# A gated MLP with adapters: gate and up by seven block products for two token tiles, samples in four quarters

## The reference

```
x = x + L0(x, itok_B_1_198)          # einsum('bct,bcd->bdt', x, weights[conditions])
x = x + L1(x, itok_B_0_7)
x = x + L2(x, itok_B_0_7) + bias
def _lora_linear(x, W, A, B, adapter_indices):
    base = jnp.einsum('bsd,df->bsf', x, W)
    lora = jnp.einsum('bsr,brf->bsf', jnp.einsum('bsd,bdr->bsr', x, Ai), Bi)
    return base + lora
h = jax.nn.silu(gate) * up           # 512 -> 2048
x = x + _lora_linear(h, Wd, Ad, Bd, adapter_indices)   # 2048 -> 512
```

## Time and profile before

| | us |
|---|---|
| median of 3 runs | 1435.89 (1435.2 to 1436.04) |
| span of the profiled execution | 1433.6 |
| TensorE busy | 1398.0 |
| DVE busy | 737.1 |
| ACT busy | 289.9 |
| POOL busy | 823.5 |

### The profile page before, as it was taken

How to read it: one execution, slowest core, us unless ns; L and a number is a source line. 1 busy time by engine, 2 the same in 40 slices (tenths; PEclk the granted TensorE clock), 3 DMA queues, 4 the chain that set the end, 5 groups by cost and what they waited for, 6 DMA issues and landing times.

```text
span 1433.6 us, 19764 instructions
## 1 busy us (share of the span) xinstructions
PE 1398.0 (98%) x6822; PEld 1177.2 (82%) x6822; DVE 737.1 (51%) x1212; ACT 289.9 (20%) x545; POOL 823.5 (57%) x854
## 2 busy tenths in 40 slices
PE   4999999999999999999989999999999999999997
PEld 4788888888888888888878888888888888888886
DVE  6885444454544545454574545445445445445456
ACT  3422211111222212122222211111111111111111
POOL 5764666666667666666642265555555555555550
PEclk7999999999999999999999999999999999999999
DMA  6522332323232232223245122222222222222213
GB/s 208 201 84 62 107 94 86 93 84 97 82 95 87 82 100 81 91 87 95 86 152 173 45 79 65 83 81 66 78 82 72 76 82 66 77 79 67 73 59 118
DMA packets 62968, 131.72 MB, mean 92 GB/s; under 512 B 13904, under 2 KB 18768, under 8 KB 62928
## 3 DMA queue, kind: packets, MB, share of 16 engines
q0 software_dynamic: 26624, 70.29, 15.5%
q1 hardware_dynamic: 36304, 60.90, 13.4%
HBM read 113.97 MB, written 17.17 MB: 91 GB/s over the span
## 4 chain that ended last, share of the span: by engine, by line
PE 94%; DVE 5%; issue 1%; DMA 0%; ACT 0%; SPq 0%; DVEq 0%; ACTq 0%
PE pd L1170 25%; PE pu L1170 25%; PE pg L1170 25%; PE pv L1170 7%; PE pu L1257 4%; PE pg L1257 3%; PE px L1170 2%; DVE acc L1058 1%; PE pu L1232 1%; DVE w_lo L884 1%; DMA bias_src<-bias_t 0%; DVE acc L1048 0%; PE px L1232 0%; DVE xt_lo L898 0%; PE pg L1311 0%
## 5 line engine op out<-in xcount | busy, mean ns | idle before, releaser
L485 POOL DMA_INDIRECT b_got<-b_table,idx_b x480 | 486.8, 1014 | 152.0 <-issue 115.7
L1027 DVE TENSOR_TENSOR h<-silu,pu 128x512 f32<-128x512 f32 x128 | 87.9, 687 | 620.3 <-PE pu L1257 620.3
L542 POOL TENSOR_TENSOR h_lo<-h,h_hi 128x512 fp32r<-128x512 f32 x128 | 166.5, 1301 | 373.6 <-ACT h_hi L648 372.4
L1058 DVE TENSOR_TENSOR acc<-pd,acc 128x512 f32<-128x512 f32 x512 | 348.4, 689 | 2.9 <-PE pd L1170 1.5
L1170 PE MATMUL pd<-w_hi,h_hi 128*128 128x512 f32 x512 | 207.2, 405 | 2.5 <-DVE acc L1058 2.5
L1170 PE MATMUL pg<-xt_hi,w_hi 128*128 128x512 f32 x528 | 208.4, 395 | 0.2 <-DVE xt_lo L898 0.2
L1170 PE MATMUL pg<-xt_hi,w_lo 128*128 128x512 f32 x528 | 206.1, 390 | 0.0
L1170 PE MATMUL pu<-xt_hi,w_hi 128*128 128x512 f32 x512 | 205.9, 402 | 0.0
L1170 PE MATMUL pg<-xt_lo,w_hi 128*128 128x512 f32 x528 | 205.9, 390 | 0.0
L1170 PE MATMUL pd<-w_lo,h_hi 128*128 128x512 f32 x512 | 200.0, 391 | 0.0
L1170 PE MATMUL pu<-xt_lo,w_hi 128*128 128x512 f32 x512 | 199.9, 390 | 0.0
(11 more groups left out here) (216 smaller groups left out, 1735.0 us busy)
## 6 DMA issues: line engine op xcount, KB each, us to landing
w_raw<-w_all SPq DMA_DIRECT2D x96, 256.0 KB, 2.7
b_got<-b_table,idx_b POOLq DMA_INDIRECT x480, 2.8
out<-acc SPq DMA_DIRECT2D x7, 1024.0 KB, 5.0
acc<-x SPq DMA_DIRECT2D x4, 1024.0 KB, 8.4
xn<-x SPq DMA_DIRECT2D x16, 256.0 KB, 2.7
x_next<-xn SPq DMA_DIRECT2D x16, 256.0 KB, 2.8
acc<-x_next SPq DMA_DIRECT2D x4, 1024.0 KB, 5.9
w_raw<-w_all SPq DMA_DIRECT2D x32, 64.0 KB, 1.9
```

What stands on the lines that cost most here:

```text
L485: gp.indirect_dma_start(out=dst, out_offset=None, in_=table, in_offset=bass.IndirectOffsetOnAxis(ap=rows.bitcast(U32), axis=0)).then_inc(s ...
L542: gp.tensor_tensor(h_lo[:, slot, :], h[:, :], h_hi[:, slot, :], ALU.subtract).then_inc(h_lo_done, 1)
L1027: dve.tensor_tensor(h[:, :], silu[:, :], pu[slot][:, :], ALU.mult).then_inc(h_done, 1)
L1058: dve.tensor_tensor(dst, psum[:, :], dst, ALU.add).then_inc(down_add, 1)
```

## The change

Samples are worked in four quarters of 8 pairs, two tiles each. A unit is one hidden block for both tiles of a quarter; the adapter products are a unit of their own (block -1), so a quarter has 17 units. Seen as 2 x 2 blocks (two tiles by two halves of the 512 inputs, times two halves by gate and up), gate and up of both tiles are eight block products. Now there are seven, made from sums and differences of token blocks (`xo_hi`, `xo_lo`: A11, S1, A12, S2, A22_T3, S3, A22) and of weight blocks (`sums` on DVE, for each unit). Some are added in PSUM (`px` takes four of them in turn), and ACT copies and DVE additions in between (`s1_kept`, `s5_kept`, `s2_kept`, `c11_done`, `u3_done`, `c12_done`, `c22_done`, `c21_kept`) form gate and up of tile 0 in `g0`, `up0` and of tile 1 in `g1`, `up1`. The products' marks p1, p5, p6, p2, p7, p3, p4 follow in this order on TensorE. Down products wait for two blocks and are added in PSUM over both: after an odd block tile 0, after the next even one tile 1, so a unit still has 30 of them and 5 additions. Weights are read and split four times instead of twice. The pairs of the next quarter are prepared in units 2 to 9 (`gather_pair`, L424 for all gathers), four turns (transposes and token sums) in units 5, 7, 9 and 11; the sums go to `xops` in DRAM and come back in unit 15. ACT waits for `b_out` (the stores of `b_table`) before the first turn of the opening. The loops are written out in full.

```diff
+QP = PAIRS // QUARTERS
+TP = QP // 2
 TOK = TP * P
...
+SUPER = BLOCKS // 2
...
+UNITS = BLOCKS + 1
...
+A11, S1, A12, S2, A22_T3, S3, A22 = range(7)
+S4 = A22_T3
...
+                if b == BLOCKS - 1 and q + 1 < QUARTERS:
+                    sp.wait_ge(xops_out, TP * (q + 1) * 16)
+                    for done, k in ((p1_mm, A11), (p5_mm, S1), (p6_mm, S2), (p2_mm, A12), (p7_mm, S3), (p3_mm, S4),
+                                    (p4_mm, A22)):
+                        sp.wait_ge(done, n + 1)
+                        for c in range(2):
+                            src = xops[:, :, k * WH + c * P:k * WH + (c + 1) * P].rearrange("j p n -> p j n")
+                            sp.dma_start(four(xo_lo[:, k, c * TOK:(c + 1) * TOK]).bitcast(F32), src
+                                         ).then_inc(xop_in[k], 16)
...
+            def gather_pair(q, i):
+                pair = (q + 1) * QP + PAIR_ORDER[i]
+                n = made(q, i)
+                gp.wait_ge(e_sum_done, n - 1)
+                gp.wait_ge(e_masked, n - 1)
+                gp.wait_ge(e_lo_done, n - 1)
+                gather_rows(ea_one[:, 0, :], w0_rows, idx_w[:, pair, 0:1], ea_got)
+                gather_rows(eb_one[:, 0, :], e_table, idx_w[:, pair, 1:2], ea_got)
...
+            for q, b in units():
+                n = unit(q, b)
+                if b == -1:
...
+                i = pair_at(q, b)
+                if i is not None:
+                    e = made(q, i)
...
+                        gather_pair(q, 0)
...
+                    gp.tensor_tensor(xn_lo[:, :], acc[:, (q + 1) % 2, PAIR_ORDER[i], :], xn_hi[:, :], ALU.subtract
+                                     ).then_inc(lx_lo, 1)
+                h_low(q, b, 0)
+                if i is not None:
+                    gp.wait_ge(f_hi_done, e)
+                    gp.tensor_tensor(bd_lo[:, :, :], em_one[:, :, :], bd_hi[:, :, :], ALU.subtract).then_inc(f_done, 1)
+                if b == BLOCKS - 1 and q + 1 < QUARTERS:
+                    token_low(q, S1)
+                if b % 2 and (q, b) != (QUARTERS - 1, BLOCKS - 1):
+                    m, to_q = ((b + 1) // 2, q) if b + 1 < BLOCKS else (0, q + 1)
...
+                    gp.wait_ge(p3_mm, n + 1)
+                    gather_b(to_q, m, 0)
+                h_low(q, b, 1)
+                if b % 2 and (q, b) != (QUARTERS - 1, BLOCKS - 1):
+                    gp.wait_ge(p4_mm, n + 1)
+                    gather_b(to_q, m, 1)
+                if b == BLOCKS - 1 and q + 1 < QUARTERS:
+                    token_low(q, A12)
+                if i is not None and i + 1 < QP:
+                    gather_pair(q, i + 1)
...
+                k = pair_at(q, b + 1)
+                if k is not None:
+                    e = made(q, k)
+                    dve.wait_ge(ea_got, e * 32)
+                    dve.wait_ge(f_done, e - 1)
+                    masked(em_one, ea_one[:, :, C:2 * C], 1).then_inc(e_masked, 1)
+                for phase_at in down_phases(q, b):
...
+                        selectors(q, 1, (0, 1))
...
+            def product(psum, k, start, stop):
+
+                for c in range(2):
+                    ws, xs = slice(c * P, (c + 1) * P), slice(c * TOK, (c + 1) * TOK)
+                    ins = split_product(psum[:, :], [w[:, k, ws] for w in (wg_hi, wg_lo)],
+                                        [s[:, k, xs] for s in (xo_hi, xo_lo)],
+                                        start=(start and c == 0), stop=(stop and c == 1), more=not start)
+                return ins
...
+            def down(q, m, t):
+                d = phase(q, m, t)
+                for half in range(2):
...
+                        else:
+                            ins = split_product(pd[j][:, :], [s[:, j * P:(j + 1) * P] for s in hs],
+                                                [w[:, half, 0:T] for w in (wd_hi, wd_lo)],
+                                                start=(half == 0), stop=(half == 1))
+                        if half:
+                            ins.then_inc(down_mm, 1)
+                        elif r == 4:
+                            ins.then_inc(down_half, 1)
+
...
-            def hidden(half, m, n, t, wslot, slot, blk, loads, selections=0, between=None):
...
-                    pe.wait_ge(*((silu_done, silus(n - 1)), (h_done, hs(n - 1)))[m])
-                split_product(psum[:, :],
-                              [lambda c, w=w: w[:, wslot, base + c * P:base + (c + 1) * P] for w in (w_hi, w_lo)],
-                              [lambda c, s=s: s[:, c, cols] for s in (xt_hi, xt_lo)],
-                              chunks=KC, close=False)
...
+                product(px, A11, True, True).then_inc(p1_mm, 1)
...
+                product(py, S1, True, True).then_inc(p5_mm, 1)
+                if k is not None:
+                    e = made(q, k)
+                    pe.wait_ge(f_done, e)
+                    pe.wait_ge(lx_lo, e)
+                    pe.wait_ge(down_add, 5 * phase(*down_phases(q, b - 1)[-1]) + 1)
+                    split_product(pd[0][:, :], [bd_hi[:, 0, :], bd_lo[:, 0, :]], [xn_hi[:, :], xn_lo[:, :]]
...
+
+                pe.wait_ge(w_done[1], n + 1)
+                pe.wait_ge(s1_kept, n + 1)
+                if adapters:
+                    tokens_ready(q, S2)
+                product(px, S2, False, True).then_inc(p6_mm, 1)
+                if i is not None:
+                    e = made(q, i)
+                    pe.wait_ge(e_lo_done, e)
+                    pe.wait_ge(down_add, 5 * (phase(*down_phases(q, b - 1)[-1]) + 1))
```

More of the change, by code:

```diff
@@ new lines, in cond_resid_kernel @@
+        eb_four = [four(stage[:, e, :]) for e in range(3)]
+        es_four = [four(stage[:, 3 + e, :]) for e in range(3)]
+        et_four = [[four(h[:, e // 2, e % 2, :]) for h in (h_hi, h_lo)] for e in range(3)]
+        ebs_four = [[four(h[:, 1, 1, e * WH:(e + 1) * WH]) for h in (h_hi, h_lo)] for e in range(2)] \
+            + [[four(b_got[:, 0, i * WH:(i + 1) * WH]) for i in range(2)]]
+        bd_four = [None] + [[four(a) for a in (v_hi[:, :], v_lo[:, :])], [four(a) for a in (xn_hi[:, :], xn_lo[:, :])]]
@@ L301, in cond_resid_kernel, with unit, phase, blocks_done @@
-        EARLY = TILES - 1
+        def unit(q, b):
+            return q * UNITS + b + 1
+        def phase(q, m, t):
+            return q * 2 * SUPER + 2 * m + t
+        def blocks_done(q, b):
+            return q * BLOCKS + b + 1
+        def made(q, i):
+            return q * QP + i + 1
+        ORDER = (0, 1, 4, 2, 3)
+        def down_bank(r):
+            return pv if ORDER[r] == 4 else pd[ORDER[r]]
+        def units():
+            for q in range(QUARTERS):
+                for b in range(-1, BLOCKS):
+                    yield q, b
@@ L457, in _ @@
+            store_y(QUARTERS - 1, 0)
+            store_y(QUARTERS - 1, 1)
+            for t in range(2):
+                for half in range(2):
+                    sp.wait_ge(y_out[half][t], 2 * 16)
             for j in range(BCH):
@@ L800, in _ @@
-            opening(OPENING)
-            act.wait_ge(bdn_in, 16)
-            copy(bdn_hi[:, :], silu[:, :]).then_inc(bdn_hi_done, 1)
-            act.wait_ge(bdn_done, 1)
-            act.sem_inc(silu_done, 1)
-            for half in range(HALVES):
-                if half:
-                    transpose(half, 0)
-                    v_high(half - 1, TILES - 1)
-                    products(half, 0)
-                early_steps(half)
-                body(half, 0, False, start=EARLY - 1)
-                with act.Fori(1, TURNS - 1) as i:
-                    body(half, i, False)
-                body(half, TURNS - 1, True)
@@ L818, in _ @@
+            for t in range(2):
+                v_high(QUARTERS - 1, t)
         @block.vector
```

1864 lines of the change are left out of this document (879 added, 985 removed).

## The result

The changed kernel takes 1675.25 us (median of 4 runs, 1671.26 to 1678.81) against 1435.55 for the kernel before (1434.97 to 1436.04): ratio 1.167, 95% interval 1.1645 to 1.1688. The forecast was 1636. The profiled execution took 1678.81 us with a span of 1676.8.

What follows compares the result with a forecast made beforehand. TensorE was taken to bound the kernel; work 1293.6 + opening 80.6 + first units 9 + pair waits 159 + low clock 24 + quarter changes 57 + end 11 = 1634 us, so 1636 as median. Range 1540 to 1690 (70%).

Steps and rivals of the forecast that it cites:

- pair waits: Units preparing next quarter's pairs: TensorE waits for late POOL gathers, 9.2 and 3.6 us in turn; 159 us with token sums.
- low clock: TensorE's slower clock after long idle: 24 us behind pair waits, 3 in the opening, 6 at quarter changes.
- Work taken away: TensorE: 408 fewer products of 0.227 us, 92.4 us less, leaving 1293.6 us; a plain unit takes 18.1 us.
- some 4 us at half speed lose 2: 12 x 2 = 24 us: Behind the 8.6 us gaps in pair units: the clock falls to the lower level, costing 24 us in all.
- Rival 3: Slower: clock stays low through most of the 24 pair units, 114 us more less 24 counted, 1720 us; chance 10%.
- Opening: Before the first unit: turns wait for b_table's stores; first unit at 90.6 us, 77.6 idle and 3 for low clock.
- Change of quarter: Three changes: token reload, low parts, selectors, u and v make TensorE wait 16.9 us each, 51 us; low clock 6.
- 7.3 us for A12 alone: At each quarter change: A12's low part, behind gathers on POOL, is ready 30 us into unit 15, wanted at 23.
- First units: Units -1, 0, 1, without down products to cover selections, silu and weight load: 9 us of waits.
- end: Kernel's close: v of both tiles masked only after the last addition, then last store; 11 us, 7.4 before.
- Rival 1: Faster: pair gathers land in time, so only opening, first units and end remain; 1353 us, chance 5%.
- POOL's low parts delayed: DVE and POOL exclude each other on SBUF: low parts on POOL delayed, estimated 10 to 20 us over the kernel.

Runs made afterwards that it cites:

- Run 10: Changed kernel with earlier pair gathers, the opening's load and quarter-change order altered, and code moved against all other waits, no work left out: 1448.0 us, ratio 1.000.
- Run 6: Changed kernel with the second half of bd_rows loaded at once into another part of stage, so b_table's stores don't queue behind its splitting: 1665.7 us, ratio 1.147.
- Runs 7 and 9: First: changed kernel with v_high, v_mask and unit 15's gathers reordered at the quarter change, 1663.6 us; second: the same with all seven low parts on DVE, 1658.8 us.
- run 2: Changed kernel with only two of four b_got row gathers per tile from the second pair of blocks on, leaving out work: 1615.2 us, ratio 1.116.

## Why the prediction was nearly right, and where it was too low

The forecast's mechanism holds, and its largest term. The total, 2.3% too low, is nearer than its terms: the pair waits were put 15 us too high and the low clock 56 too low. By its own steps, measured in the profiled execution (span 1676.8 against 1634):

- **Work taken away.** 408 products, as counted (x6822 to x6414). A unit without pairs takes 18.17 us (1434.47 to 1452.64), against 18.1.
- **Pair waits: 159 predicted, 143.8 measured.** In the windows of the pairs and of the turns 46.3 + 47.7 + 44.5 and 3 x 1.8 us are idle. The first two long waits of a quarter are 8.7 and 8.9 (8.6 predicted), at the instructions named: before px in unit 2, before pd in 4, 6 and 8. But units 6 and 8 wait 6.5 and 6.4 (4.9 and 4.7 in the third quarter), I take it because the turn's wait in the unit before holds TensorE while POOL goes on; no run shows it. Odd units wait 2.0 to 2.9 instead of 3.6. The turns wait 1.84 us each, not 0.4: 22 against 5.
- **Low clock: 33 predicted, about 89 measured. This is the term that was mis-sized.** Cut into windows of 4 us, the execution gives in each a busy time of TensorE and a granted clock; busy time multiplied by what the clock lacks to 1.00 sums to 89 us, an estimate: 12 in the opening, 10 in the first units, 38 in the pair units, 26 at the three changes, 3 else. The step "some 4 us at half speed lose 2: 12 x 2 = 24 us" holds: behind the twelve long waits it is 27.6 us, 2.3 each. What failed is that the clock was counted there and almost nowhere else: 3 us for the opening (12), nothing for the first units (10), 6 for the changes (26), nothing for the odd units and the turns (10.7 in the pair units, and the 3 else). In the odd units the clock can fall behind short waits in a row, as in the timeline of TensorE in unit 3 of the first quarter:

```profile
188.96 0.47 PE L1097 MATMUL pd<-xn_hi,bd_hi 128*128 128x512 f32 x1 [0.93 <-DVE acc L932]
190.58 0.47 PE L1097 MATMUL px<-xo_hi,wg_hi 128*128 128x512 f32 x1 [0.70 <-ACT g L556]
193.58 0.42 PE L1097 MATMUL pd<-eb_hi,et_hi 128*128 128x64 f32 x1 [0.79 <-POOL eb_lo L523]
```

  and the window behind them:

```profile
192.00:196.00 4.00, 3.21 (x9) 2.20 (x9) 3.50 (x6) 1.11 (x2) 1.99 (x4) 0.50 0.57 162
```

  It doesn't always fall there. Unit 3 of the second quarter has nearly the same waits (0.81, 0.69 and 1.40 us), and the clock stays at 1.00:

```profile
606.58 0.47 PE L1097 MATMUL px<-xo_hi,wg_hi 128*128 128x512 f32 x1 [0.69 <-ACT g L556]
609.59 0.30 PE L1097 MATMUL pd<-eb_hi,et_hi 128*128 128x64 f32 x1 [1.40 <-POOL eb_lo L523]
...
608.00:612.00 4.00, 2.60 (x15) 2.15 (x15) 3.50 (x6) 1.11 (x2) 2.00 (x4) 1.00 0.53 162
```

  Rival 3 had this mechanism and put 114 us on the pair units; it is 38, for even behind the 8.67 us wait of unit 2 the starts are 0.43 apart only from 167.84 to 170.53, and 0.23 from 171.29 on. Run 10 checks the size: the same 6414 products are busy 1332.9 us there against 1400.3 to 1405.0, 67 to 72 less, and the same arithmetic gives 24 us there, 65 less.
- **Opening: first unit at 90.6 predicted, 98.40 measured.** The stores went out from 52.03 rather than 49.6 and landed after a median 9.8 us rather than 6.8, and the turns stand 7.34 us apart instead of 6.7. Run 6 confirms that the stores set the start.
- **Change of quarter: 51 predicted, 49.5 idle measured,** but 7.3 us for A12 alone was the wrong cause, and that the total came out is in part luck (the terms listed also add up to 16.75 for each change, not 16.9). A12's wait is 2.50; 4.92 stand before S2, where ACT's `v_high` waits for DVE's `v_mask`, which is behind a low part stretched to 2.80 us. Undoing both showed the next holder, the shared stretching of DVE and POOL.
- **First units 9 predicted, 5.3 idle; end 11 and 10.0.**
- **Rival 1's time was added up wrong.** Its 47.6 us are the idle time and warm-up of the kernel before (35.6 + 12.0). With the opening, first units and end of the forecast itself (80.6 + 9 + 11) it would have been 1394 us, not 1353. The forecast doesn't rest on it.

Step by step, the measured span less the forecast: opening +7.8, its low clock counted apart -3, first units -3.7, pair waits -15, changes and end -1.5 and -1, last quarter +1.2, low clock from the first unit on (77 against 30) +47, the rest of the work at full clock +11; together 43. These 11 us I did not trace. They lie in TensorE's busy time: without the low clock, by the same arithmetic in both kernels, it fell from 1391.9 to 1315.8 us, by 76 instead of 92.4. The Trainium skill (SBUF — State Buffer, Who interferes with whom) says that a DVE operation with two SBUF inputs and a GpSimd operation that reads SBUF exclude each other. Runs 7 and 9 agree, with 2.56 against 0.42 us for the same subtraction. The prediction saw POOL's low parts delayed by it; what held TensorE up was the delay of DVE.

## What to carry to other kernels

Before a table of gathers is made longer on a queue, look at what stands at the queue's end and who waits for it: POOL stood idle for 2.9 to 3.8 us ahead of each pair unit's first `h_lo`, and moving two gathers there was worth 128 us. Price a wait of the matrix engine with the clock behind it; here 161 us of idle time taken away brought 67 us of busy time along. A change that saves some 7% of the product time (92.4 of 1386 us) paid here only after most of its waits were gone: the same seven products gave a ratio of 1.167 with 272 us idle and 0.991 with 97.

## What the runs showed of the hardware

DVE instructions with two operands in SBUF stretched beside a POOL subtraction, and POOL's too: `g<-g,up` 2.88 us against 0.69, `w_raw` 2.56 against 0.41, `xo_lo` on DVE 3.40 against 1.2, and on POOL 2.83 each against 2.34 in the changed kernel, beside a less busy DVE. Gathers of `b_got` rows of 512 columns land after a median 3.9 us. A gather of `eb_one` landed after 2.3 to 2.5 us, and after 3.9 to 4.6 where the DMA engines were nearly full (run 2). The kernel before took 0.5 to 1.1% longer on the four other chips; the changed one, timed on one of them, did not.
